# Moving two quarters of the position products, the last keys' projection and the axis exchange between two images of a hybrid attention kernel

## The chip, the cores and the metric

The kernel runs on one core of one Trainium2 chip. The metric is the device time of one execution in microseconds (us); the time given for a kernel is the median of its runs.

## The reference, cut to what matters

Eight images of 32 x 32 positions with 384 channels pass through two layers. Layer 0 is attention over all 1024 positions of an image with six heads of 64, with a position term for rows and one for columns added to the scores; layer 1 is causal attention and a feed-forward. The part that the change touches is layer 0's:

```
x = x + _L0_conv_ref(_gn(x), ...)
qkv = x.reshape(b, hw, c) @ qkv_w + qkv_b
attn = jnp.einsum('bqd,bkd->bqk', q * SCALE, k)
rel_h = jnp.einsum('bhwc,hkc->bhwk', r_q, Rh)
rel_w = jnp.einsum('bhwc,wkc->bhwk', r_q, Rw)
attn = attn + rel_h[:, :, :, :, None] + rel_w[:, :, :, None, :]
attn = jax.nn.softmax(attn, axis=-1)
```

and, at the end of an image, the feed-forward of layer 1:

```
h = x @ w_fc.T
h = jax.nn.gelu(h, approximate=False)
out = h @ w_proj.T
```

## The kernel before, in words

The order of the work is written out by hand, one instruction list for each engine, with semaphores between them. The eight images go one after the other. Matrices are kept as a float16 high part and a float16 low part, so most products are three matmuls.

One image is: position and value products of layer 0, its attention, its output projection, the normalisation and projections of layer 1, its attention, its output projection, and the feed-forward. The next image's layer 0 projections of queries and keys are laid into the feed-forward of this one, because there the tensor engine would wait for the gelus. This stretch between two attentions, called the seam here, occurs seven times.

In the seam the work before the change is this.

- `pair_products` (L555) makes two heads' queries or keys: 18 matmuls of 512 columns into two banks of PSUM. There are six pairs, 0 to 2 queries and 3 to 5 keys. Pairs 0 to 2 come before the feed-forward's twelve steps, pairs 3 to 5 are cut in pieces of five matmuls (`FILL`) and put one piece behind each `up` (L1303). ScalarE takes a pair out as its high part (`pair_high`, L574, two instructions), VectorE as its low part (`pair_low`, L591, two instructions).
- `turn_all` (L617) on GpSimd makes copies of the queries with the image's two axes exchanged: 12 instructions, which start when both parts of a pair are there.
- The feed-forward: `up`, `gelu` (L1315) on ScalarE, `down` (L1323), then for either half `o2_out` (L1329, VectorE), `spread` (L1337, PE), two `widen` (L1352, VectorE) and two `add` (L1358, GpSimd).
- `rel_products` (L653) are the position products, in four quarters of 96 small matmuls. Each quarter is taken out by four `rel_high` (L670) on ScalarE and four `rel_low` (L676) on VectorE. The first quarter waits for the low parts of all six pairs, and one quarter is put behind each of the value products 0 to 3.
- `v_products` (L688, L693) are the values, eight tiles of nine matmuls and a bias; `v_high` (L700, L701) on ScalarE and `v_low` (L705) on GpSimd take them out.
- The largest scores of head 0: 16 products `use("max", 0, n)` (L825), each followed by a reduction on VectorE (`release`, L971). They wait for 14 of the 16 `rel_low`, and use four banks in turn. Then `combine` (L1006, VectorE) puts the two halves together, a small matmul (L830) and a copy (L979) turn the result to a row, and a DMA (L1063) puts it beside the queries.
- Behind the row's matmul stand the last value product, the last two `rel_low`, and then the scores (`score_tiles`, L861, L863, L872) and the exponentials (L947), which begin the attention proper.

The exponential needs another table in ScalarE than the gelu. It is loaded where the first exponential stands.

Of the kernel before, what the change touches and what calls it, by code (L numbers as in the profile page):

```python
# [514 lines left out]
class Projections:  # L515

    COUNTS = (dict(mm=6, hi=12, lo=12, turned_hi=6, turned_lo=6, rel_mm=4, rel_hi=16, rel_lo=16, v_mm=8, v32=8, v_lo=8), dict(mm=6, hi=12, lo=12, v_mm=8, v32=8, v_lo=8))
# [60 lines left out]
    def pair_low(self, dve, i, heads=(0, 1)):  # L578
        nc, m, s, layer = self.nc, self.m, self.s, self.layer
        f = self.order[i]  # L580
        for e in heads:
# [17 lines left out]
            last.then_inc(s["lo"], 1)  # L599

    def copy_queries(self, sp, p):
# [28 lines left out]

    def rel_out(self, n):

        return self.m.ps[:, 2 * (1 - n % 2):2 * (1 - n % 2) + 2, :].rearrange("p k (i c) -> p (k i) c", c=P)[:, :, 0:NPAIR * IMG]

    def rel_products(self, pe, n):

        nc, m, s = self.nc, self.m, self.s
        if n >= 2:
            pe.wait_ge(s["rel_lo"], s.at("rel_lo", 4 * (n - 1)))
# [72 lines left out]
class Attention:  # L712
# [6 lines left out]
    def __init__(self, nc, m, layer, s, proj, norm=None, next_in=None):  # L719
# [47 lines left out]
        self.beside_v = (0, 0, 0, 2, 8, 14, 20, 25, len(self.prologue)) if self.causal else (0, 0, 0, 0, 0, 0, 6, len(self.prologue))  # L767
# [7 lines left out]
        ahead = (4, 5, 0, 1, 2, 3) if self.causal else (4, 5, 2, 3)  # L775
        self.banks = [ahead[r % len(ahead)] if r < len(self.prologue) else 4 + r % 2 for r in range(len(self.index))]
# [69 lines left out]
    def score_tiles(self, pe, i):  # L846
# [5 lines left out]
        sl = slot(h)  # L852
        if i >= 2:
# [15 lines left out]
        if g == 0:  # L869
            pe.wait_ge(s["row"], s.at("row", 16 * (h + 1)))  # L870
        for j in range(2):
# [67 lines left out]

    def scalar(self, act):  # L940
        nc, m, s = self.nc, self.m, self.s
        for i in range(self.N):
            w = self.cols(i)
            act.wait_ge(s["scores"], s.at("scores", i + 1))
            if i >= RING:
# [427 lines left out]
def build(nc, x, qkv_w, qkv_b, proj_w, proj_b, rel_h, rel_w, wq, wk, wv, wo, bo, c_fc_1, c_fc_2, c_proj_1, c_proj_2, out):  # L1373
# [7 lines left out]
    with ExitStack() as ctx:  # L1381
# [11 lines left out]
        ff_s = Counters(nc, ctx, "ff", **FeedForward.COUNTS)  # L1393
        copies_s = Counters(nc, ctx, "copies", queries=16 * NH)
        work = []
        for b in range(images):
# [3 lines left out]
            if b:  # L1400
                w.qkv0.copied = copies_s.of(b - 1)
            if b == 0:
                w.qkv0.bank, w.qkv0.before = (6, 4, 2, 0, 4, 2), (0, 0, 0, 0, 4, 6)
            w.with_v = ((0,), (1,), (2,), (3,), (), (), (), ()) if b else ((), (), (0,), (1,), (2,), (3,), (), ())
# [12 lines left out]
        REL_ORDER = list(range(16))  # L1417
# [4 lines left out]
        FILL = (0, 5, 5, 5, 5, 5, 5, 5, 5, 5, 5, 4)  # L1422
        HIGHS = (1, 2, 4, 5, 8, 9, 11, 11)
# [3 lines left out]
        def tensor(pe, w, before):  # L1427
            qkv0, attn0, proj0, ln, qkv1, attn1, proj1, ff = w.qkv0, w.attn0, w.proj0, w.ln, w.qkv1, w.attn1, w.proj1, w.ff
            for t in range(NT - 1):
                if not before or t > 0:  # L1430
                    qkv0.v_products(pe, t)
                for n in w.with_v[t]:
                    if n == 0:
                        pe.wait_ge(qkv0.s["lo"], qkv0.s.at("lo", 2 * PAIRS))
                    if before and n == 1:
                        pe.wait_ge(before.ff.s["widened"], before.ff.s.at("widened", 4))
                    qkv0.rel_products(pe, n)
                if t == 5 and not before:
                    prologue.ready(pe)
                if t == 5:  # L1440
                    pe.wait_ge(qkv0.s["rel_lo"], qkv0.s.at("rel_lo", RELS - 2))
                for u in attn0.prologue_part(t):
                    attn0.use(pe, u)
# [211 lines left out]
```

## Time and profile before

| | |
|---|---|
| median of three runs | 2883.28 us (2877.95 to 2890.47) |
| the profiled execution | 2876.72 us |
| its span | 2874.7 us |
| TensorE busy | 2648.2 us (92%) |
| VectorE busy | 1987.1 us (69%) |
| ScalarE busy | 2047.1 us (71%) |
| GpSimd busy | 1734.9 us (60%) |

Busy times are from the profile's page. Matmuls overlap in it, so 92% doesn't mean that TensorE works at its peak. The profile is of one execution, which was the shortest of those shown here, 6.6 us under the median. L with a number is a line of the kernel before; PE, DVE, ACT, POOL and SP are TensorE, VectorE, ScalarE, GpSimd and the queue that issues the DMAs.

### The profile page before, as it was taken

What the parts mean: (1) busy time and instruction counts of PE and PEld (TensorE: products, weight loads), DVE (VectorE), ACT (ScalarE), POOL (GpSimd) and SP (SyncE); (2) the same over time, 40 slices, a digit from 0 to 9 for tenths busy, and PEclk for the clock granted to TensorE, in tenths of its full rate; (3) what the DMA queues carried; (4) which work ended last, traced back from release to release, by engine and by line L of the source; (5) the groups of instructions that cost most, each with busy time, mean ns of one, the idle gap of its engine ahead of it and who ended that gap; (6) DMA issues with size and microseconds to landing.
All of it is one profiled execution on the core that took longest, in us unless ns stands there. A gap on an engine that the chain in (4) does not pass through costs nothing.

```text
span 2874.7 us, 69176 instructions
## 1 busy us (share of the span) xinstructions
PE 2648.2 (92%) x29116; PEld 1548.0 (54%) x29116; DVE 1987.1 (69%) x3631; ACT 2047.1 (71%) x2435; POOL 1734.9 (60%) x1181
## 2 busy tenths in 40 slices
PE   7899998999989998999989999899998999989995
PEld 4465644656446563565635656366553655546562
DVE  7776767666775767757677576775777758677574
ACT  6686866858668586785767867678766777668683
POOL 5474764737657376573756746566565665657473
PEclk8999999999999999999999999999999999999998
DMA  3100011000100001000010000200002000010000
GB/s 113 36 2 1 2 34 45 2 1 2 56 23 2 1 2 56 23 2 1 2 57 23 2 1 6 74 2 2 1 9 71 2 2 1 12 45 2 1 2 22
DMA packets 36115, 53.65 MB, mean 19 GB/s; under 512 B 5824, under 2 KB 32704, under 8 KB 35808
## 3 DMA queue, kind: packets, MB, share of 16 engines
q1 hardware_dynamic: 34304, 48.64, 5.5%
q8 instruction: 231, 3.78, 0.5%
q10 hardware_dynamic: 1504, 0.61, 0.1%
q14 instruction: 76, 0.62, 0.1%
HBM read 30.95 MB, written 12.58 MB: 15 GB/s over the span
## 4 chain that ended last, share of the span: by engine, by line
PE 49%; POOL 16%; ACT 13%; issue 11%; DVE 9%; DMA 1%; POOLq 0%; ACTq 0%; DVEq 0%; SPq 0%
POOL pl L1013 15%; PE ps L555 12%; PE ps L902 7%; PE ps L688 4%; PE ps L861 4%; PE ps L872 4%; ACT p L947 4%; PE ps L825 4%; PE ps L1104 4%; DVE mxp L971 3%; PE ps L863 3%; ACT ph L933 3%; ACT qa L670 2%; PE ps L1303 2%; PE ps L1323 2%
## 5 line engine op out<-in xcount | busy, mean ns | idle before, releaser
L1013 POOL TENSOR_TENSOR pl<-p,ph 128x1024 f16<-128x1024 f32 (+2 forms) x672 | 1095.9, 1644 | 384.2 <-ACT ph L933 378.3
L971 DVE TENSOR_REDUCE mxp<-ps 128x1 f32<-128x512 f32 (+2 forms) x1344 | 779.4, 627 | 267.9 <-PE ps L825 263.3
L947 ACT ACTIVATE p<-ps 128x1024 f32<-128x1024 f32 (+1 forms) x672 | 640.3, 953 | 165.8 <-PE ps L872 165.0
L933 ACT ACTIVATE ph<-p 128x1024 f16<-128x1024 f32 (+1 forms) x672 | 669.3, 996 | 21.4
L902 PEld LDWEIGHTS ps<-v,ph 128*128 128x128 f16 x9600 | 506.2, 97 | 128.2 <-issue 27.6
L902 PE MATMUL ps<-v,ph 128*128 128x65 f16 (+1 forms) x9600 | 531.0, 194 | 17.0 <-POOL pl L1013 16.0
L902 PE MATMUL ps<-v,pl 128*128 128x65 f16 x4800 | 509.1, 192 | 0.0
L902 PEld LDWEIGHTS ps<-v,pl 128*128 128x128 f16 x4800 | 446.8, 99 | 0.0
L872 PE MATMUL ps<-qc,kc 65*128 65x512 f16 (+3 forms) x1344 | 380.0, 364 | 0.1
L1013 DVE TENSOR_TENSOR pl<-p,ph 128x512 f16<-128x512 f32 (+1 forms) x336 | 244.2, 727 | 184.3 <-ACT ph L933 183.0
L705 POOL TENSOR_TENSOR v<-o,v 128x384 f16<-128x384 f32 x128 | 116.7, 918 | 411.0 <-ACT o L701 411.0
L861 PE MATMUL ps<-qa,ka 128*128 128x512 f16 x768 | 292.5, 381 | 0.0
L863 PE MATMUL ps<-qb,ka 128*128 128x512 f16 x768 | 291.7, 380 | 0.0
L825 PE MATMUL ps<-ka,qa 128*128 128x512 f16 x768 | 247.1, 383 | 43.9 <-DVE mxp L971 25.1
L700 ACT ACTIVATE v<-ps 128x384 f16<-128x384 f32 x128 | 63.6, 497 | 180.8 <-PE ps L693 107.3
L872 PEld LDWEIGHTS ps<-qc,kc 65*128 65x128 f16 (+1 forms) x1344 | 123.8, 98 | 126.4 <-issue 0.5
L825 PEld LDWEIGHTS ps<-ka,qa 128*128 128x128 f16 x768 | 73.2, 97 | 182.7 <-DVE mxp L971 70.8
L861 PE MATMUL ps<-qa,qb 128*128 128x512 f16 (+1 forms) x576 | 162.0, 344 | 2.1 <-ACT p L947 2.1
L555 PE MATMUL ps<-xin,wqkv_hi 128*128 128x512 f16 x576 | 155.9, 384 | 4.0 <-DVE xin L508 2.2
L825 PE MATMUL ps<-qb,qa 128*128 128x512 f16 (+2 forms) x576 | 154.9, 325 | 0.0
L1000 DVE TENSOR_TENSOR lT<-ps,hT 128x512 f16<-128x512 f32 x96 | 66.4, 692 | 127.5 <-ACT hT L938 127.5
L1315 ACT ACTIVATE p<-ps 128x1024 f32<-128x1024 f32 x96 | 98.0, 1021 | 60.6 <-PE ps L1303 59.5
(187 smaller groups left out, 5075.2 us busy)
## 6 DMA issues: line engine op xcount, KB each, us to landing
xin<-in_x SPq DMA_DIRECT2D x8, 1536.0 KB, 6.9
x<-in_x SPq DMA_DIRECT2D x8, 1536.0 KB, 8.1
out<-x SPq DMA_DIRECT2D x16, 768.0 KB, 4.1
qc<-qa SPq DMA_DIRECT2D x42, 128.0 KB, 2.3
p<-in_L_conv_qkv_w SPq DMA_DIRECT2D x3, 576.0 KB, 10.6
qc<-rowt SPq DMA_DIRECT2D x96, 2.0 KB
x<-in_L_attn_Wq SPq DMA_DIRECT2D x1, 576.0 KB, 7.9
x<-in_L_attn_Wk SPq DMA_DIRECT2D x1, 576.0 KB, 9.0
```

The lines of the kernel that those rows point to most:

```text
L555: mm = nc.tensor.matmul(m.ps[:, self.bank[i] + j, :], w[:, k, self.order[i] * P:(self.order[i] + 1) * P], x(k, 4 * j, 4 * j + 4), start=(n ...
L688: mm = nc.tensor.matmul(m.ps[:, 6 + t % 2, 0:C], flat_tile(x(k, t, t + 1)), w[:, k, 2 * C:3 * C], start=(n == 0), stop=(self.layer == 1 an ...
L705: self.nc.gpsimd.tensor_tensor(self.m.v[:, t, :, HD + 1:VW], self.m.o[:, t, :].rearrange("p (h d) -> p h d", d=HD), self.m.v[:, t, :, 0:HD ...
L825: mm = nc.tensor.matmul(m.ps[:, bank, 0:w], m.qa[:, sl, qt * P:(qt + 1) * P], self.ka[:, sl, kh * BANK:kh * BANK + w], start=not diag, sto ...
L861: nc.tensor.matmul(outs[j], self.ka[:, sl, keys[j]], m.qa[:, sl, q], start=True, stop=False)
L863: nc.tensor.matmul(outs[j], self.ka[:, sl, keys[j]], m.qb[:, sl, q], start=False, stop=False)
L872: mm = nc.tensor.matmul(outs[j], m.kc[crows(h), sl, keys[j]], m.qc[crows(h), sl, q], start=False, stop=True)
L902: mm = nc.tensor.matmul(m.ps[:, 6 + half % 2, c0:c0 + w], e, v, start=(first and n == 0), stop=(g in self.last_of_half and n == len(work) ...
L933: self.nc.scalar.activation(m.ph[:, i % RING, :, 0:w], m.p32[:, i % RING, :, 0:w], ACT.Copy).then_inc(self.s["hi"], 1)
L947: nc.scalar.activation(m.p32[:, i % RING, :, 0:w], m.ps[:, 2 * (i % 2):2 * (i % 2) + 2, 0:w], ACT.Exp, scale=SCALE).then_inc(s["exp"], 1)
L971: nc.vector.reduce_max(m.mxp[:, h % 2, kh, qt:qt + 1], m.ps[:, bank, 0:w], AX.X).then_inc(s["free"], 1)
L1013: engine.tensor_tensor(m.pl[:, i % RING, part, 0:w], m.p32[:, i % RING, part, 0:w], m.ph[:, i % RING, part, 0:w], ALU.subtract).then_inc(s ...
```

## The change

1. Pair 5 (the keys of heads 4 and 5) leaves the feed-forward. Its 18 matmuls are put, two at a time, behind the first nine of head 0's products for the largest scores, and value product 5 behind the next three. `FILL` has four matmuls a step in place of five, nine times.
2. ScalarE takes pair 5 out twice: as high part, and whole in float32 into a piece of `p32` that the exponentials don't use yet. GpSimd subtracts the two (two instructions) for the low part, behind `v_low` 5. The second scores wait until the bank is read, the fourth exponential and heads 4 and 5 until the low part is there.
3. Quarters 0 and 1 of the position products go into the feed-forward's end, with banks of their own. The first value product's pieces move ahead too. Quarters 2 and 3 follow value products 1 and 2. ScalarE's `rel_high` 0 to 3 and VectorE's `rel_low` 0 to 3 move with them.
4. The largest scores of head 0 use two banks in place of four, begin after 12 `rel_low`, and stand together. Value product 6 comes behind them, in the first image too.
5. `turn_all` starts when the layer's last small normalisation is done, and goes by the high parts first.
6. The first `spread` stands a step earlier; the exponential's table is asked for behind `v_high` 4.

```
-        self.bank = (4, 6, 2, 4, 2, 4) if layer == 0 else (0, 2, 4, 6, 0, 2)
-        self.before = (0, 0, 0, 2, 6, 8) if layer == 0 else (0, 0, 0, 0, 2, 4)
+        self.bank = (4, 6, 2, 4, 2, 2) if layer == 0 else (0, 2, 4, 6, 0, 2)
+        self.before = (0, 0, 0, 2, 6, 0) if layer == 0 else (0, 0, 0, 0, 2, 4)
+        self.late = None
...
+    def last_keys_out(self, act):
+
+        i = 2 * NPAIR - 1
+        f = self.order[i]
+        self.pair_high(act, i)
+        self.nc.scalar.activation(self.held_keys(), self.out2(i), ACT.Identity, bias=self.m.bqk[:, f:f + 1]).then_inc(self.late["whole"], 1)
+
+    def held_keys(self):
+        return self.m.p32[:, RING - 1, :, :].rearrange("p a b -> p (a b)")
+
+    def last_keys_low(self, pool, done):
+        m = self.m
+        pool.wait_ge(self.late["whole"], self.late.at("whole", 1))
+        pool.wait_ge(self.s["v_lo"], self.s.at("v_lo", done))
+        for h in (NH - 2, NH - 1):
+            self.nc.gpsimd.tensor_tensor(m.kc[own(h), slot(h), :], self.held_keys()[own(h), :], self.ka[own(h), slot(h), :],
+                                         ALU.subtract).then_inc(self.s["late_lo"], 1)
+        pool.wait_ge(self.s["late_lo"], self.s.at("late_lo", 2))
...
-        for p in range(NPAIR):
-            pool.wait_ge(s["lo"], s.at("lo", 2 * p + 2))
-            for part in range(2):
-                for parity in range(2):
-                    self.turn(pool, part, p, parity)
+        for part, p in ((0, 0), (0, 1), (1, 0), (1, 1), (0, 2), (1, 2)):
+            ready = ("hi", "lo")[part]
+            pool.wait_ge(s[ready], s.at(ready, 2 * p + 2))
+            for parity in range(2):
+                self.turn(pool, part, p, parity)
...
-        ahead = (4, 5, 0, 1, 2, 3) if self.causal else (4, 5, 2, 3)
-        self.banks = [ahead[r % len(ahead)] if r < len(self.prologue) else 4 + r % 2 for r in range(len(self.index))]
+        ahead = (4, 5, 0, 1, 2, 3) if self.causal else (0, 1)
+        first = len(self.prologue) + (not self.causal)
+        self.banks = [ahead[r % len(ahead)] if r < first else 4 + r % 2 for r in range(len(self.index))]
...
-            w.with_v = ((0,), (1,), (2,), (3,), (), (), (), ()) if b else ((), (), (0,), (1,), (2,), (3,), (), ())
+            w.with_v = ((1,), (2,), (3,), (), (), (), (), ()) if b else ((), (), (0,), (1,), (2,), (3,), (), ())
...
-        FILL = (0, 5, 5, 5, 5, 5, 5, 5, 5, 5, 5, 4)
-        HIGHS = (1, 2, 4, 5, 8, 9, 11, 11)
+        FILL = (0, 4, 4, 4, 4, 4, 4, 4, 4, 4, 0, 0)
+        HIGHS = (1, 2, 5, 6, 9, 10)
+        BESIDE_MAX = 9
...
+            pe.wait_ge(qkv0.s["rel_hi"], qkv0.s.at("rel_hi", RELS))
+            pe.wait_ge(qkv0.s["rel_lo"], qkv0.s.at("rel_lo", RELS - 4))
+            for u in attn0.prologue:
+                attn0.use(pe, u)
+                n = u[2]
+                if before and n < BESIDE_MAX:
+                    qkv0.pair_products(pe, PAIRS - 1, part=(EACH * n // BESIDE_MAX, EACH * (n + 1) // BESIDE_MAX))
+                elif before and n < BESIDE_MAX + NC_:
+                    qkv0.v_products(pe, NT - 3, [n - BESIDE_MAX])
+            qkv0.v_products(pe, NT - 2)
...
+                if i == 10 and w.next:
+                    pe.wait_ge(ff.s["widened"], ff.s.at("widened", 2))
+                    after.v_products(pe, 0, range(NC_ - 1))
+                if i == 11 and w.next:
+                    pe.wait_ge(after.s["lo"], after.s.at("lo", 2 * PAIRS - 4))
+                    after.rel_products(pe, 0)
...
-                if i == 9:
+                if i == 8:
                     ff.spread(pe, 0)
             if w.next:
-                pe.wait_ge(ff.s["widened"], ff.s.at("widened", 2))
-                after.v_products(pe, 0, range(NC_ - 1))
+                after.v_products(pe, 0, range(NC_ - 1, NC_))
             ff.down(pe, ff.PAIRS - 1)
             if w.next:
-                after.v_products(pe, 0, range(NC_ - 1, NC_))
+                pe.wait_ge(after.s["lo"], after.s.at("lo", 2 * PAIRS - 2))
+                after.rel_products(pe, 1)
             ff.spread(pe, 1)
...
+                if t == 4:
+                    attn0.table(act)
+                    if before:
+                        qkv0.last_keys_out(act)
...
-            low(4, (0,))
             ff.widen(dve, 0)
             ff.widen(dve, 1)
-            low(4, (1,))
-            low(5, (0,))
+            low(4)
             ff.o2_out(dve, 1)
-            low(5, (1,))
+            if w.next:
+                w.next.qkv0.rel_low(dve, 0)
             ff.widen(dve, 2)
             ff.widen(dve, 3)
+            if w.next:
+                for r in range(1, 4):
+                    w.next.qkv0.rel_low(dve, r)
```

## Rows read from the trace of the kernel before

**Rows 1.** The chain that ended last, first seam: start us, length us, what.

```profile
418.91 0.69 issue
...
420.94 1.23 PE ps L653 x96
...
439.79 1.46 PE ps L688 x9
441.25 0.27 PE ps L693
...
448.88 2.99 PE ps L688 x9
451.88 0.43 PE ps L693
```

**Rows 2.** The timeline of ACT, first seam: start us, length us, engine, line, operation.

```profile
422.20 3.28 ACT L670 ACTIVATE qa<-ps 32x768 f16<-32x768 f32 x4 [1.62 <-PE ps L653]
...
453.23 1.28 ACT L947 ACT_TABLE_LOAD   x1
454.53 1.02 ACT L947 ACTIVATE p<-ps 128x1024 f32<-128x1024 f32 x1
```

**Rows 3.** The timeline of DVE, same stretch.

```profile
421.79 0.95 DVE L1352 TENSOR_TENSOR pl<-ps,cp 128x768 f32<-128x768 f32 x1
423.03 3.91 DVE L676 TENSOR_TENSOR qb<-ps,qa 32x768 f16<-32x768 f32 x4 [0.29 <-ACT qa L670]
...
438.05 9.90 DVE L971 TENSOR_REDUCE mxp<-ps 128x1 f32<-128x512 f32 x16 [0.49 <-PE ps L825]
447.99 0.17 DVE L1006 TENSOR_TENSOR mxp<-mxp 128x8 f32<-128x8 f32 x1
448.92 0.28 DVE L979 CAST rowt<-ps 8x128 f16<-8x128 f32 x1 [0.77 <-PE ps L830]
```

**Rows 4.** The timeline of PE, same stretch, from a feed-forward step to the scores.

```profile
412.55 0.60 PE L1303 MATMUL ps<-ph,c 96*128 96x512 f16 x2
...
419.62 1.08 PE L1337 MATMUL ps<-spread,pl 128*128 128x32 f32 x8
...
439.40 0.39 PE L825 MATMUL ps<-ka,qa 128*128 128x512 f16 x1 [0.21 <-DVE mxp L971]
...
452.24 0.58 PE L861 MATMUL ps<-qa,ka 128*128 128x512 f16 x1
```

**Rows 5.** The chain again, one feed-forward step: `down`, `up`, five matmuls of a pair.

```profile
406.37 1.00 PE ps L1323 x8
...
407.90 1.08 PE ps L555 x5
```

**Rows 6.** The timeline of POOL, first and last of six pairs of `turn`.

```profile
391.88 3.93 POOL L617 TENSOR_SCALAR hT<-qa 64x1024 f16<-64x1024 f16 x2 [7.36 <-DVE qb L591]
...
411.84 3.92 POOL L617 TENSOR_SCALAR lT<-qb 64x1024 f16<-64x1024 f16 x2
```

**Rows 7.** Windows, PE alone: stretch, length, busy, granted clock (1.00 is full), DMA, GB/s.

```profile
428.00:430.00 2.00, 1.42 (x98) 1.00 0.39 136
444.00:446.00 2.00, 1.37 (x4) 0.96 0.00 0
...
446.00:453.00 7.00, 4.75 (x16) 0.52 0.00 0
...
2555.40:2562.40 7.00, 4.75 (x17) 0.76 0.01 3
```

**Rows 8.** The timelines of POOL and DVE inside the attention, 467 to 471 us.

```profile
467.68 2.13 POOL L1013 TENSOR_TENSOR pl<-p,ph 128x1024 f16<-128x1024 f32 x1 [1.37 <-ACT ph L933]
468.23 1.60 DVE L1006 TENSOR_TENSOR mxp<-mxp 128x8 f32<-128x8 f32 x1
```

**Rows 9.** The timeline of PE in the third seam, a stop inside a quarter.

```profile
1129.46 0.21 PE L653 MATMUL ps<-qa,rel_lo 64*32 64x96 f16 x1 [1.53 <-issue]
```

More of the change, by code:

```diff
@@ L598, in pair_low @@
                 last = nc.vector.tensor_copy(self.ka[other(h), slot(h), :], src[own(h), slot(h), :])
-            last.then_inc(s["lo"], 1)
+            if layer == 0 and i == 2 * NPAIR - 1:
+                last.then_inc(s["late_lo"], 1)
+            else:
+                last.then_inc(s["lo"], 1)
     def copy_queries(self, sp, p):
@@ L852, in score_tiles @@
         sl = slot(h)
+        if i == 1 and self.layer == 0 and self.proj.late:
+            pe.wait_ge(self.proj.late["whole"], self.proj.late.at("whole", 1))
         if i >= 2:
@@ L870, in score_tiles @@
             pe.wait_ge(s["row"], s.at("row", 16 * (h + 1)))
+        if g == 0 and self.layer == 0 and h == NH - 2:
+            pe.wait_ge(self.proj.s["late_lo"], self.proj.s.at("late_lo", 2))
         for j in range(2):
@@ L938, in ot_high, with table @@
         self.nc.scalar.activation(self.m.hT[:, c, hf * BANK:(hf + 1) * BANK], self.m.ps[:, self.bank(u), :], ACT.Copy).then_inc(self.s["ot_hi"], 1)
+    def table(self, act):
+        self.nc.scalar.activation(self.m.idle[:, :], self.m.bqk[:, 0:1], ACT.Exp, scale=0.0)
     def scalar(self, act):
@@ L944, in scalar @@
             act.wait_ge(s["scores"], s.at("scores", i + 1))
+            if i == RING - 1 and self.layer == 0 and self.proj.late:
+                act.wait_ge(self.proj.s["late_lo"], self.proj.s.at("late_lo", 2))
             if i >= RING:
@@ L1428, in tensor @@
             qkv0, attn0, proj0, ln, qkv1, attn1, proj1, ff = w.qkv0, w.attn0, w.proj0, w.ln, w.qkv1, w.attn1, w.proj1, w.ff
-            for t in range(NT - 1):
+            for t in range(NT - 3):
                 if not before or t > 0:
@@ L1433, in tensor @@
                     if n == 0:
-                        pe.wait_ge(qkv0.s["lo"], qkv0.s.at("lo", 2 * PAIRS))
+                        pe.wait_ge(qkv0.s["lo"], qkv0.s.at("lo", 2 * PAIRS - 2))
+                        pe.wait_ge(qkv0.s["late_lo"], qkv0.s.at("late_lo", 2))
                     if before and n == 1:
+                        continue
+                    if before and n == 2:
                         pe.wait_ge(before.ff.s["widened"], before.ff.s.at("widened", 4))
                     qkv0.rel_products(pe, n)
[L1438 to L1443, printed above, removed]
+            if not before:
+                prologue.ready(pe)
+                qkv0.v_products(pe, NT - 3)
+                qkv0.rel_products(pe, 3)
+            pe.wait_ge(qkv0.s["rel_hi"], qkv0.s.at("rel_hi", RELS))
[8 more added lines that the diff above has]
+            qkv0.v_products(pe, NT - 2)
             def beside_row():
@@ L1525, in scalar, with vector @@
                         w.next.qkv0.pair_high(act, 2 + n // 2, (n % 2,))
-        def vector(dve, w):
+            if w.next:
+                for r in range(4):
+                    w.next.qkv0.rel_high(act, r)
+        def vector(dve, w, before):
             qkv0, attn0, proj0, ln, qkv1, attn1, ff = w.qkv0, w.attn0, w.proj0, w.ln, w.qkv1, w.attn1, w.ff
-            for r in REL_ORDER[:-2]:
+            for r in range(4 if before else 0, RELS - 2):
                 qkv0.rel_low(dve, r)
@@ L1534, in after_row @@
             def after_row():
-                for r in REL_ORDER[-2:]:
+                for r in range(RELS - 2, RELS):
                     qkv0.rel_low(dve, r)
@@ L1569, in gpsimd @@
                 qkv0.v_low(pool, t)
+                if t == 5 and before:
+                    qkv0.last_keys_low(pool, t + 1)
             attn0.gpsimd(pool, proj0.bias_tiles)
@@ L1612, in _ @@
                 prologue.scalar(act)
-                for w in work:
-                    scalar(act, w)
+                for b, w in enumerate(work):
+                    scalar(act, w, work[b - 1] if b else None)
             @block.vector
@@ L1618, in _ @@
                 prologue.vector(dve)
-                for w in work:
-                    vector(dve, w)
+                for b, w in enumerate(work):
+                    vector(dve, w, work[b - 1] if b else None)
             @block.gpsimd
@@ L1624, in _ @@
                 prologue.gpsimd(pool)
-                for w in work:
-                    gpsimd(pool, w)
+                for b, w in enumerate(work):
+                    gpsimd(pool, w, work[b - 1] if b else None)
             @block.sync
```

21 lines of the change are left out of this document (13 added, 8 removed).

## The prediction

> **What bounds the kernel now.** I read the profile's page first: PE is busy 92% of the span, so a saving has to come from stretches in which PE waits. The change touches the seam between two images, so I followed the chain of waits through the first seam, 390 to 460 us, and then laid the engines' timelines beside each other. The other six seams look alike; three of them lose another 0.4 to 1 us in the position products.
>
> The chain leaves PE at 420.9. Quarter 0 of the position products takes 1.23 us to its first reader [rows 1], and from then on ScalarE goes without a gap until 438.07: four `rel_high` of 0.82 us and a value tile of 0.9 us make 4.2 us a quarter, four times [rows 2]. VectorE follows 0.3 us behind, does its 14th `rel_low` at 437.57, and starts the 16 reductions at 438.05 [rows 3]. They take 9.90 us, one every 0.61 us. In them PE does one matmul for each and waits for VectorE [rows 4], and its granted clock falls from 1.00 to 0.50 (2.4 to 1.2 GHz) at 446 us: a mean of 0.52 over the next 7 us [rows 7]. So value product 7 takes 2.99 + 0.43 us, where value product 5 needs 1.46 + 0.27 us at the full clock [rows 1]. The scores begin at 452.24 [rows 4], the first exponential at 454.53, held by the table load that ends there [rows 2]. The reader should see three things in turn: ScalarE's 16.8 us, VectorE's 9.9 us, and PE at half speed.
>
> **The feed-forward's end.** Nine steps lose a matmul: five take 1.08 us [rows 5], so nine are 1.94 us. Steps with a `down` are bound by PE and keep that gain; steps without are bound by the round `up`, gelu, `up` of 1.71 us (412.55 to 414.26) and PE now waits 0.2 us in them. `up` 10, at 412.55 before [rows 4], comes at 410.6 to 410.8. `up` 11 follows 1.71 us later, at 412.4. Then PE has 0.43 (`up`), 1.1 (quarter 0), 1.0 (`down` [rows 5]), 0.7 (the rest of value product 0), 1.0 (`down`), 1.1 (quarter 1), and comes to the second `spread` at 417.75, before at 419.62 [rows 4]: 1.9 us earlier, although two quarters now lie ahead of it. One reason is that the stop of 0.69 us for `o2_out` [rows 1] is filled by quarter 1. The earlier first `spread` costs nothing: its `o2_out` is done 0.5 us before.
>
> Are quarter 0's inputs there at 412.8? `turn_all` waited 7.36 us for `pair_low` and ran from 391.88 to 415.76, 12 x 1.99 us [rows 6]. It now starts at 386.1, when the small normalisation is done, and ends at 410.0. That is 2.8 us before quarter 0, so the earlier start is needed and is just enough. It has no price on VectorE, whose instructions there read PSUM.
>
> **The position products.** ScalarE begins them at about 414.6 and has its 16 `rel_high` and three value tiles done at 430.7, no longer the bound. VectorE is: one `rel_low` lies before the last two `widen`, which end at 420.85 (before 422.74 [rows 3]); 13 more at 3.91 / 4 = 0.98 us [rows 3] end at 433.6. The reductions start at 433.65 in place of 438.05: **4.4 us**.
>
> **The largest scores.** With two banks product n waits for reduction n-2. From a reduction's end to PE's start are 0.13 us and the product takes 0.39 us [rows 4], together under the 0.61 us of a reduction, so two banks alone cost nothing. But PE now has three matmuls of 0.216 us a step, 0.65 us, seven times; then three steps with a third of value product 5, 2.4 us; then four at 0.61 us. Set out from the first reduction, the last ends at 10.55 us, not 9.90. Value product 6 runs from 9.7 to 11.4, so the row's matmul waits for it until 11.4 (in place of 10.3). Copy until 12.1, two `rel_low` of 0.98 us until 14.05, and the scores start at **14.05**; value product 7, at the full clock, is done at 13.4 under them. Before it was 452.24 - 438.05 = 14.19 us. The scores' first half also ran at the slow clock, 0.3 us. The table load is under cover; since the scores' later steps follow PE and not the first exponential, its 0.6 us count for nothing. Sum with nothing in the way: 4.4 + 0.1 + 0.3 = **4.8 us a seam**.
>
> **What is in the way.** *The clock.* PE is idle from 429.0 to 431.8 and from 433.1 to 434.4, waiting for `rel_low`. Before, PE was busy 1.42 of 2 us there [rows 7] and kept the full clock; the clock fell behind the reductions, with PE busy 1.37 of 2 us and then waiting for `combine` [rows 7]. I expect it to fall as the reductions start. At half clock a step is 1.30 us, not 0.65, so each slow microsecond costs half of one. Means of 0.52 and 0.76 over 7 us [rows 7] are 6.8 and 3.4 us at half clock in the first and the last seam, and part of the new one lies in PE's idle time. Bounds 0 and 3.4 us; I take **0.85 us** for 1.7 us of exposure.
>
> *The port.* Pair 5 is out of PE 5.3 us behind the first reduction. ScalarE then has 1.11 + 1.13 + 1.1 us and the value tile 0.97, until 9.8; GpSimd `v_low` 5 until 10.7, and then the two new subtractions of some 2.1 us each (2.13 us for 128 x 1024 [rows 8]). `combine` is due at 10.6. Inside the attention `combine`, 0.17 us alone [rows 3], began at 468.23 while GpSimd subtracted two SBUF operands, and ended with it: 1.60 us [rows 8]. So `combine` waits for `v_low` 5 or, if it comes a few tenths late, for the first new subtraction, until 12.9: 1.8 us on the path. My walk isn't good to 0.2 us; I take half, **0.9 us**, with bounds 0 and 1.8.
>
> The Trainium skill, "SBUF — State Buffer", section "Who interferes with whom", gives a rule for this: a VectorE instruction with two SBUF inputs and a GpSimd one that reads SBUF shut each other out for a whole instruction, and the first to start wins. By that rule a seam gains either 3.95 or 2.15 us and nothing between, as one engine or the other comes first. The trace agrees: `combine` ended when GpSimd did [rows 8].
>
> Late keys elsewhere: GpSimd ends them at 15.0 and its last `v_low` at 16.8, before the first exponentials' low part is due (about 17.7); the fourth exponential is due later still. The second scores wait for ScalarE's third reading at 8.8, done. On SP nothing changes its order: the query copies still follow `pair_high`, and the stores and the load of x come 2 us earlier. The last image has no next one to fill its feed-forward; there only the first `spread` moves, ahead of work that waits for gelus, so its end stays.
>
> *The first image* has no products beside its reductions: it starts them when it did, but value product 6 now stands between them and the row instead of among them. At the clock that fell there it takes 3.4 us, partly beside the last reduction; on the other side a gap of 0.6 us among the reductions goes. I take 0.7 us lost, bounds -1 and 1.5.
>
> **Sum.** 4.8 - 0.85 - 0.9 = 3.05 us a seam, 21.4 us in seven, less 0.7: 20.7 us. From the profiled 2876.7 us that is 2856; the median stands 6.6 us above that execution, so 2862.6 for a median like it. I give 2861. What a measurement of this kernel can tell from no change is about 0.5%, 14.4 us.
>
> **Rivals.**
> - *Clean*: PE keeps its clock and `combine` comes first. 7 x 4.8 - 0.7 = 33 us, 2850 us (2844 beside the profiled execution). For it: PE is full once the reductions run. Against: 4 us of idle time just before. Chance 0.2.
> - *Port every time*: `combine` always meets the new subtraction: 7 x 2.15 - 0.7 = 14.4 us, 2869 us. For it: the schedule repeats, so it may well be all seven or none. Chance 0.2.
> - *Quarters that stop*: PE stood 1.53 us inside a quarter in the third seam, waiting for nothing the profile shows [rows 9]. Two quarters now lie on PE's way to the last `spread`, and through `widen` on VectorE's. Two such stops a seam take 3 us, which with the clock leaves less than 1 us a seam: 2878 us, no change. Against: only three seams showed stops, all late in the stretch. Chance 0.12, with whatever else hides the gain.
> - *Slower*: the clock stays low from the first reduction to the scores. Ten steps then take 13.8 us, not 6.9, value products 6 and 7 3.4 us each, and the scores start 24 us behind the first reduction: 10 us lost against 4.8 won, 7 x 5.2 = 37 us, 2920 us. It decides from 9.6 us of slow clock on. Against it: the longest such stretch is 6.8 us, and PE is busy throughout. Chance 0.05.
>
> The forecast itself has 0.43. Faster by over 0.5% are it, clean, and two thirds of the port case: 0.76; within 0.5% 0.19; slower 0.05. The range takes in clean, from 2845, and reaches to the port case with a slow clock of full length, 2875.
>
> **What would show it.** Right: first reduction about 15 us behind the second `spread`, not 18; 16 reductions in 10.5 to 12 us; a `combine` of 0.2 to 2.1 us; value product 7 in 1.7 us; no table load before the first exponential. Wrong: gaps on VectorE between `rel_low`s (then ScalarE or PE bounds), PE waiting for `turn` at quarter 0, a granted clock of 0.50 beyond 5 us in the reductions, or `combine` late for value product 5.

## The result, and the profile after

The changed kernel takes 2852.81 us (median of four runs, 2849.44 to 2853.7), the kernel before beside it on the same chip 2880.61 (2876.35 to 2890.47): a ratio of 0.9899 with a 95% interval of 0.9881 to 0.9917. The forecast was 2861 us in a range of 2845 to 2875, faster with a chance of 0.76. It came out faster by 1.0%, inside the range and 8 us below the forecast. The two profiled executions have spans of 2874.7 and 2849.7 us: 25.0 us less, where the steps of the forecast summed to 20.7.

The page's first part, of the kernel after:

```profile
span 2849.7 us, 69244 instructions
...
PE 2638.5 (93%) x29116; PEld 1547.0 (54%) x29116; DVE 1973.6 (69%) x3617; ACT 2058.2 (72%) x2450; POOL 1763.1 (62%) x1195
```

Busy times have hardly moved: PE has 10 us less, GpSimd 28 us more (the late keys' subtractions). What went is waiting. The timeline of ACT in the first seam (start us, length us, engine, line; L695 is `rel_high`, L617 the late keys' second reading, L983 the exponential):

```profile
414.73 3.28 ACT L695 ACTIVATE qa<-ps 32x768 f16<-32x768 f32 x4
...
427.34 3.28 ACT L695 ACTIVATE qa<-ps 32x768 f16<-32x768 f32 x4
...
432.31 1.28 ACT L972 ACT_TABLE_LOAD   x1
...
439.74 2.24 ACT L575 ACTIVATE ka<-ps,bqk 64x1024 f16<-64x1024 f32 x2 [5.94 <-PE ps L556]
442.01 1.11 ACT L617 ACTIVATE p<-ps,bqk 128x1024 f32<-128x1024 f32 x1
...
449.94 1.02 ACT L983 ACTIVATE p<-ps 128x1024 f32<-128x1024 f32 x1 [0.98 <-PE ps L902]
...
453.23 1.02 ACT L983 ACTIVATE p<-ps 128x1024 f32<-128x1024 f32 x1 [1.17 <-PE ps L902]
```

ScalarE starts its 16 readings 7.5 us earlier than in [rows 2] and is done at 430.62, 3.4 us ahead of the reductions. The table load stands before the late keys' reading, and the first exponential now waits for PE, not for it. The timeline of DVE, same stretch (L701 is `rel_low`, L1007 the reductions, L1042 `combine`, L1015 the row's copy):

```profile
417.95 0.95 DVE L701 TENSOR_TENSOR qb<-ps,qa 32x768 f16<-32x768 f32 x1
...
420.21 0.95 DVE L1388 TENSOR_TENSOR pl<-ps,cp 128x768 f32<-128x768 f32 x1
421.19 12.79 DVE L701 TENSOR_TENSOR qb<-ps,qa 32x768 f16<-32x768 f32 x13
434.01 8.04 DVE L1007 TENSOR_REDUCE mxp<-ps 128x1 f32<-128x512 f32 x12
442.44 2.48 DVE L1007 TENSOR_REDUCE mxp<-ps 128x1 f32<-128x512 f32 x4 [0.38 <-PE ps L851]
444.95 0.17 DVE L1042 TENSOR_TENSOR mxp<-mxp 128x8 f32<-128x8 f32 x1
446.25 0.28 DVE L1015 CAST rowt<-ps 8x128 f16<-8x128 f32 x1 [1.13 <-PE ps L856]
```

The 13 `rel_low` run back to back: VectorE is the bound, as the working said. The first reduction starts at 434.01, before at 438.05 [rows 3]; the 16 take 10.91 us, before 9.90. GpSimd's timeline (L640 the turn, L730 `v_low`, L627 the late keys' subtractions) shows how close the port came:

```profile
387.25 7.87 POOL L640 TENSOR_SCALAR hT<-qa 64x1024 f16<-64x1024 f16 x4 [1.64 <-issue]
...
407.22 3.92 POOL L640 TENSOR_SCALAR lT<-qb 64x1024 f16<-64x1024 f16 x2
...
443.96 0.88 POOL L730 TENSOR_TENSOR v<-o,v 128x384 f16<-128x384 f32 x1 [10.63 <-ACT o L726]
444.99 4.32 POOL L627 TENSOR_TENSOR kc<-p,ka 64x1024 f16<-64x1024 f32 x2
```

`combine` began at 444.95, the subtraction at 444.99. It came 0.04 us ahead and took 0.17 us, in this seam and in the other six. That is a fixed distance, not the same near miss seven times: in six traces whose order of work is the same here (the changed kernel twice, and the runs below with the quarters back, the old turn, the late table load and the filler) it is 0.03 or 0.04 us in all 42 seams, while `combine` itself comes anywhere from 10.71 to 13.39 us behind the first reduction. In these traces both sides follow PE: ScalarE starts its readings when the late keys' last matmul is done and GpSimd follows ScalarE, and the 13th reduction waits 0.38 us for a product that stands behind value product 5. No run moved the one without the other to test this, except the delayed `combine` below. PE, the quarter's first matmul, the row's and the scores' first:

```profile
413.11 0.22 PE L678 MATMUL ps<-qa,rel_hi 64*32 64x96 f16 x2
...
445.83 0.39 PE L856 MATMUL ps<-minus,mxp 128*8 128x128 f32 x2
...
448.43 0.39 PE L889 MATMUL ps<-qa,ka 128*128 128x512 f16 x1 [0.39 <-DVE qb L701]
```

**Where the 25 us are.** I cut each seam at three marks that both traces have: the narrow input of the next image's projections (`x2_high`), the first reduction, and the second exponential of the first head. Means over the seven seams, in us, from the timelines:

| | before | after | gained, all seams |
|---|---|---|---|
| narrow input to first reduction | 52.89 | 49.53 | 23.5 |
| first reduction to second exponential | 18.87 | 19.31 | -3.0 |
| the rest of the image | six 279.9, last 268.2 | six 279.1, last 267.9 | 5.0 |
| first image, to its narrow input | 384.33 | 385.43 | -1.1 |
| behind the last narrow input | 40.3 | 39.7 | 0.6 |

That sums to 25.0. The third line was in no step of the forecast. It is the clock. The table is of one execution of each kernel, and the first image alone is not sure to 2 us: in a second trace of the changed kernel it takes 387.72 us. Other executions of the kernel before lose more clock: on one chip they go from 2874.17 us at a granted clock of 0.982 to 2888.29 at 0.973, the changed kernel's beside them only from 2848.87 to 2854.46 at 0.982 to 0.980. So in the difference of the medians, 27.8 us, the clock has probably a larger part than here; no run separates it. Windows of PE alone, after (stretch, length, busy, granted clock, DMA, GB/s):

```profile
432.00:436.00 4.00, 3.86 (x11) 0.59 0.46 163
436.00:443.00 7.00, 6.61 (x33) 1.00 0.00 0
443.00:450.00 7.00, 6.22 (x32) 1.00 0.11 15
739.60:743.00 3.40, 3.40 (x10) 0.58 0.00 0
780.60:784.00 3.40, 3.40 (x11) 0.58 0.32 112
```

and before:

```profile
798.00:805.00 7.00, 5.17 (x17) 0.55 0.01 2
955.00:959.00 4.00, 3.66 (x14) 0.65 0.02 4
```

Before, the clock fell to 1.2 GHz behind the reductions (3.4 us in five seams, 6.8 in two, as 798 to 805) and again some 218 us behind the narrow input, in the second layer (955), in all images but the last. After, both are gone. In their place it falls as the reductions start (432, 780), and in six of seven seams also some 7 us behind the narrow input (739.6), where before it did so in the first seam only. The second trace of the changed kernel has the same two low stretches in the same seams, and none at 218 us.

### The profile page after: what moved, and what is told of

It reads as the page before. It is cut to its first block, busy times and chain, and to the rows that moved or that the text cites. A ratio compares the mean times of both kernels' runs of the same rounds, so it can differ in the third digit from the quotient of the medians.

```text
span 2849.7 us, 69244 instructions
## 1 busy us (share of the span) xinstructions
PE 2638.5 (93%) x29116; PEld 1547.0 (54%) x29116; DVE 1973.6 (69%) x3617; ACT 2058.2 (72%) x2450; POOL 1763.1 (62%) x1195
## 4 chain that ended last, share of the span: by engine, by line
PE 51%; POOL 16%; ACT 12%; issue 11%; DVE 10%; DMA 0%; POOLq 0%; ACTq 0%; DVEq 0%; SPq 0%
POOL pl L1049 15%; PE ps L556 12%; PE ps L932 7%; PE ps L851 5%; PE ps L889 4%; PE ps L902 4%; PE ps L713 4%; ACT p L983 4%; PE ps L1140 4%; DVE qb L701 3%; PE ps L891 3%; ACT ph L963 3%; PE ps L1339 2%; ACT p L1351 2%; PE ps L1359 2%
## 5 line engine op out<-in xcount | busy, mean ns | idle before, releaser
L1007 DVE TENSOR_REDUCE mxp<-ps 128x1 f32<-128x512 f32 (+2 forms) x1344 | 784.0, 626 | 258.8 <-PE ps L851 253.0
L983 ACT ACTIVATE p<-ps 128x1024 f32<-128x1024 f32 (+1 forms) x672 | 641.0, 954 | 175.8 <-PE ps L902 175.0
L730 POOL TENSOR_TENSOR v<-o,v 128x384 f16<-128x384 f32 x128 | 116.1, 918 | 369.3 <-ACT o L726 368.7
L851 PE MATMUL ps<-ka,qa 128*128 128x512 f16 x768 | 260.5, 392 | 54.9 <-DVE mxp L1007 22.3
L556 PE MATMUL ps<-xin,wqkv_hi 128*128 128x512 f16 x576 | 167.5, 404 | 2.5 <-DVE xin L508 2.2
```

Source lines behind the costliest of these rows:

```text
L556: mm = nc.tensor.matmul(m.ps[:, self.bank[i] + j, :], w[:, k, self.order[i] * P:(self.order[i] + 1) * P], x(k, 4 * j, 4 * j + 4), start=(n ...
L730: self.nc.gpsimd.tensor_tensor(self.m.v[:, t, :, HD + 1:VW], self.m.o[:, t, :].rearrange("p (h d) -> p h d", d=HD), self.m.v[:, t, :, 0:HD ...
L851: mm = nc.tensor.matmul(m.ps[:, bank, 0:w], m.qa[:, sl, qt * P:(qt + 1) * P], self.ka[:, sl, kh * BANK:kh * BANK + w], start=not diag, sto ...
L983: nc.scalar.activation(m.p32[:, i % RING, :, 0:w], m.ps[:, 2 * (i % 2):2 * (i % 2) + 2, 0:w], ACT.Exp, scale=SCALE).then_inc(s["exp"], 1)
L1007: nc.vector.reduce_max(m.mxp[:, h % 2, kh, qt:qt + 1], m.ps[:, bank, 0:w], AX.X).then_inc(s["free"], 1)
```

## The experiments

Each is the changed kernel with one edit, unless it says otherwise. "R0" is the first reduction.

**Quarters 0 and 1 back behind the last `spread`**, with everything else of the change kept.

```diff
-            w.with_v = ((1,), (2,), (3,), (), (), (), (), ()) if b else ((), (), (0,), (1,), (2,), (3,), (), ())
+            w.with_v = ((0,), (1,), (2,), (3,), (), (), (), ()) if b else ((), (), (0,), (1,), (2,), (3,), (), ())
...
-                    after.rel_products(pe, 0)
...
-                after.rel_products(pe, 1)
...
-                for r in range(4):
-                    w.next.qkv0.rel_high(act, r)
...
-            for r in range(4 if before else 0, RELS - 2):
+            for r in range(RELS - 2):
...
-                w.next.qkv0.rel_low(dve, 0)
...
-                for r in range(1, 4):
-                    w.next.qkv0.rel_low(dve, r)
```

> The changed kernel with the two quarters of the position products put back behind value products 0 and 1; the late keys and the rest stay. My theory (the start of the reductions sets the gain, and ScalarE's 16 rel_high of 0.82 us in a row bound it as before): ScalarE begins its first rel_high behind the second spread, at about 420 us of the first seam and not at 414.7, the reductions start 3.1 us later than in the changed kernel, 7 x 3.1 = 22 us more, span about 2871 us. Rival (the gain is from pair 5 being out of the feed-forward, the quarters only follow it): under 1 us a seam, span 2850 to 2856 us.

Median 2875.1 us, ratio to before 0.9984 (0.9974 to 0.9994), span 2870.7: 21.0 us above the changed kernel. The total is as forecast, its make-up is not: the start of the reductions was to come 3.1 us later a seam and came 1.2 later, which is 8.3 us of the 21.0. Timeline of DVE, first seam:

```profile
430.16 1.95 DVE L701 TENSOR_TENSOR qb<-ps,qa 32x768 f16<-32x768 f32 x2 [0.29 <-ACT qa L695]
...
433.26 0.69 DVE L1007 TENSOR_REDUCE mxp<-ps 128x1 f32<-128x512 f32 x1 [1.15 <-PE ps L851]
434.54 0.69 DVE L1007 TENSOR_REDUCE mxp<-ps 128x1 f32<-128x512 f32 x1 [0.59 <-PE ps L851]
```

`rel_low` follows `rel_high` again (0.29 us), and the first reductions wait 1.15 and 0.59 us for PE, which was idle for 4.69 us ahead of them (2.87 in the changed kernel): in six seams its clock is then low for 6.8 us, not 3.4. R0 is at 50.71 against 49.53, and the second exponential comes another 1.6 us later behind it (20.90 against 19.31): 11.1 us in seven seams. What is left against before is 4 us in all. R0 itself is still 2.2 us a seam ahead of the kernel before; the wait for PE and the longer low stretch behind it give nearly all of that back. So without the two quarters, the rest of the change is worth next to nothing in time.

**The last keys' projection back at the feed-forward's end**, quarters kept, their banks changed over and the waits to match.

```diff
-        self.bank = (4, 6, 2, 4, 2, 2) if layer == 0 else (0, 2, 4, 6, 0, 2)
+        self.bank = (4, 6, 2, 4, 2, 4) if layer == 0 else (0, 2, 4, 6, 0, 2)
...
-        FILL = (0, 4, 4, 4, 4, 4, 4, 4, 4, 4, 0, 0)
-        HIGHS = (1, 2, 5, 6, 9, 10)
-        BESIDE_MAX = 9
+        FILL = (0, 5, 5, 5, 5, 5, 5, 5, 5, 5, 5, 4)
+        HIGHS = (1, 2, 4, 5, 8, 9, 11, 11)
+        BESIDE_MAX = 0
...
-                    if before:
-                        qkv0.last_keys_out(act)
...
-                    qkv0.last_keys_low(pool, t + 1)
...
+            low(5)
```

> The changed kernel with pair 5 back in the feed-forward (five matmuls a step again, its low part on VectorE), and the two quarters still at the feed-forward's end, their banks changed over so that quarter 0 needs pairs 0 to 4 only and quarter 1 all six. My theory: PE has 18 x 0.216 = 3.9 us more before the second spread, less the 0.2 us stops in four steps, and VectorE two pair_low of 1.29 us; the 16 reductions take 10.3 us and not 10.9. Sum 2.5 to 3.5 us a seam, 18 to 25 us more, span 2868 to 2874 us. Rival (the matmuls of pair 5 cost as much beside the reductions as in the feed-forward, so its place is worth nothing): 0 to 0.5 us a seam.

Median 2878.24 us, ratio 0.9999 (0.9986 to 1.0012), span 2879.1: 29.4 us above the changed kernel, more than forecast. R0 is 2.0 us later a seam, 14.1 us in all, as the filled steps say. Another 4.7 us come between R0 and the second exponential, 7.0 in the rest of the images and 3.6 in the first image and at the end; for the most part that is the clock. Without the late keys' matmuls between the largest scores PE waits 0.21 us or more ahead of each of the last ten products. Timeline of DVE, first seam:

```profile
441.93 8.06 DVE L1007 TENSOR_REDUCE mxp<-ps 128x1 f32<-128x512 f32 x13 [0.90 <-PE ps L851]
...
452.54 0.28 DVE L1015 CAST rowt<-ps 8x128 f16<-8x128 f32 x1 [2.34 <-PE ps L856]
```

The clock is low at the reductions' start in all seams and again behind them in five, and at 218 us (207 in the last image) in the second layer in all. With the clock low behind the reductions the row's copy waits 2.34 us, in this seam, and the rest of the image is 1.0 us longer in the mean. So both parts are needed: the quarters alone, like the keys alone, leave the kernel within 0.2% of before.

**The turn in its old order**, `pair_low` waited for pair by pair.

```diff
-        for part, p in ((0, 0), (0, 1), (1, 0), (1, 1), (0, 2), (1, 2)):
-            ready = ("hi", "lo")[part]
-            pool.wait_ge(s[ready], s.at(ready, 2 * p + 2))
-            for parity in range(2):
-                self.turn(pool, part, p, parity)
+        for p in range(NPAIR):
+            pool.wait_ge(s["lo"], s.at("lo", 2 * p + 2))
+            for part in range(2):
+                for parity in range(2):
+                    self.turn(pool, part, p, parity)
```

> The changed kernel with the exchange of axes in its old order, each pair waiting for its low part. My theory: the 12 turns run from 392.9 (the first pair's low part) for 12 x 1.99 us until 416.8, not until 411.1, quarter 0 waits for them from 413.1 to 416.9, and all behind it on PE is 3.8 us later: 7 x 3.8 = 27 us more, span about 2876 us, no better than the kernel before. Rival (quarter 0 has slack, because ScalarE or VectorE bound what follows): under 1.5 us a seam.

One execution: 2898.43 us, span 2896.7, 47 us above the changed kernel, where 27 were forecast. The turn begins 5.6 us later (392.90) and quarter 0 waits for it. Timeline of PE:

```profile
416.99 0.22 PE L678 MATMUL ps<-qa,rel_hi 64*32 64x96 f16 x2 [4.01 <-POOL lT L640]
```

R0 is 4.9 us later a seam (54.44), 1.5 later than in the kernel before, for 3.8 forecast. I had not counted that PE, idle for four microseconds, loses its clock: a further low stretch lies some 32 us behind the narrow input in every seam, of 3.4 us in five and of 6.8 in two. The early turn is what makes the early quarters possible.

**Combine a little later**: two small reductions ahead of it, with no use but time.

```diff
+        if h == 0 and self.layer == 0:
+            for j in range(2):
+                nc.vector.reduce_max(m.rs[:, 1, j:j + 1], m.mxp[:, 0, 1, 0:4], AX.X)
         nc.vector.tensor_tensor(m.mxp[:, h % 2, 0, both], m.mxp[:, h % 2, 0, both], m.mxp[:, h % 2, 1, both], ALU.max).then_inc(s["combined"], 1)
```

> The changed kernel with two small reductions (0.17 us each) ahead of head 0's combine on VectorE, so that GpSimd's first subtraction of the late keys, which started 0.04 us behind combine, starts before it. My theory (the two lock each other out for a whole instruction): combine takes about 2 us, the row's matmul comes 1.3 to 1.5 us later, 9 to 12 us more in all, span 2859 to 2862 us. Rival (no lock; only the added 0.34 us, which value product 6 on PE covers): combine stays at 0.17 us and the span within 1.5 us of 2849.7.

One execution: 2886.86 us, span 2885.1: 35 us lost, not 9 to 12. The lock itself is as forecast. Timeline of DVE, and behind it of POOL:

```profile
448.05 0.22 DVE L1044 TENSOR_REDUCE rs<-mxp 128x1 f32<-128x4 f32 x2
448.19 2.04 DVE L1045 TENSOR_TENSOR mxp<-mxp 128x8 f32<-128x8 f32 x1
450.79 0.28 DVE L1015 CAST rowt<-ps 8x128 f16<-8x128 f32 x1 [0.56 <-PE ps L856]
```

```profile
448.08 4.31 POOL L627 TENSOR_TENSOR kc<-p,ka 64x1024 f16<-64x1024 f32 x2
```

`combine` is now 0.11 us behind the subtraction and takes 2.04 us in all seven seams, not 0.17. The rule quoted ahead from the Trainium skill, "SBUF — State Buffer", section "Who interferes with whom", agrees with this: the first to start keeps the other out for its whole instruction, and `combine` ends when the subtraction does. Beside `combine`, part of value product 6 was waited for anyway (1.13 us ahead of the copy in the changed kernel, 0.56 here), so the copy comes 1.5 to 1.6 us later in the three seams where the low stretch lies about as it did: 10 to 11 us in seven. The other 24 are the clock, as far as they can be placed. In three seams the low stretch at the reductions grows to 6.8 us and the copy comes at 16.0 instead of 13.9; the rest of the image is 8.2 us longer in all; and the last image's feed-forward runs at 1.2 GHz to the end, 7.8 us more. The first image is 3.1 us longer, but of that 2.3 us lie between two traces of the changed kernel too. With a single execution, how much of the 24 the delay brought on is not shown. Windows of PE:

```profile
2834.80:2884.00 49.20, 28.71 (x96) 0.50 0.08 30
```

**Value products 5 and 6 spread out among the reductions**, 16 of the late keys' matmuls put into PE's wait for the last `rel_low`, and GpSimd held after the subtractions until `combine` is done.

```diff
-        BESIDE_MAX = 9
+        AHEAD = 16
+        V5, V6 = (2, 4, 7), (9, 11, 13)
...
+            if before:
+                pe.wait_ge(qkv0.s["rel_lo"], qkv0.s.at("rel_lo", 8))
+                qkv0.pair_products(pe, PAIRS - 1, part=(0, AHEAD))
...
-                if t == 5 and before:
+                if t == 4 and before:
                     qkv0.last_keys_low(pool, t + 1)
+                    pool.wait_ge(attn0.s["combined"], attn0.s.at("combined", 1))
```

> The changed kernel with its second stretch laid out by what the traces showed: 16 of pair 5's 18 matmuls go into the 2.9 us in which PE waits for rel_low ahead of the reductions, the last two behind product 0, a third of value product 5 behind products 2, 4 and 7, a third of value product 6 behind 9, 11 and 13; GpSimd makes the late keys' low part ahead of v_low 5, and v_low 5 to 7 wait for combine. My theory: PE has no idle stretch ahead of the reductions, so the clock stays at 1.00 there; they take 10.0 us, not 11.0, combine meets no subtraction, the row's matmul waits for nothing, and the row's copy comes at 10.8 us behind the first reduction, not at 12.35. 1.5 us a seam and as much in the first image: span about 2838 us. Rival (the clock's low stretches move with any change of the period, as in the kernel with the later combine, and cost elsewhere what they leave here): the span within 5 us of 2849.7 or above, with low stretches at other places of each image.

Median 2846.93 us (2842.22 to 2853.26), ratio 0.9871 (0.9853 to 0.9889), span 2843.8, 5.9 us below the changed kernel but not the 2838 expected. Timelines of DVE and of POOL in the second seam:

```profile
788.39 1.29 DVE L1007 TENSOR_REDUCE mxp<-ps 128x1 f32<-128x512 f32 x2 [0.28 <-PE ps L851]
789.72 0.17 DVE L1042 TENSOR_TENSOR mxp<-mxp 128x8 f32<-128x8 f32 x1
790.44 0.28 DVE L1015 CAST rowt<-ps 8x128 f16<-8x128 f32 x1 [0.56 <-PE ps L856]
```

```profile
782.18 4.31 POOL L627 TENSOR_TENSOR kc<-p,ka 64x1024 f16<-64x1024 f32 x2 [3.82 <-ACT p L617]
790.01 1.74 POOL L730 TENSOR_TENSOR v<-o,v 128x384 f16<-128x384 f32 x2 [3.52 <-DVE mxp L1042]
```

GpSimd's subtractions end 3.2 us before `combine`, and the row waits 0.56 us, not 1.13, since no value product stands whole ahead of it. The second exponential comes at 18.40 in six seams (19.55 in one), 0.7 us sooner in the mean than the changed kernel's 19.31. The low stretch at the reductions is gone, and that at 7 us is left in two seams; one at some 213 us (203 in the last image) is back in five of seven, and the rest of the images is 5.1 us longer for it. That is what the rival foretold in part. The edit has three parts, and this run does not tell them apart.

**Only the 12 matmuls in the gap**, three steps of two more, nothing else moved.

```diff
-        BESIDE_MAX = 9
+        AHEAD = 12
+        BESIDE_MAX = 3
...
+            if before:
+                pe.wait_ge(qkv0.s["rel_lo"], qkv0.s.at("rel_lo", 8))
+                qkv0.pair_products(pe, PAIRS - 1, part=(0, AHEAD))
...
-                    qkv0.pair_products(pe, PAIRS - 1, part=(EACH * n // BESIDE_MAX, EACH * (n + 1) // BESIDE_MAX))
+                    qkv0.pair_products(pe, PAIRS - 1, part=(AHEAD + 2 * n, AHEAD + 2 * n + 2))
```

> The changed kernel with 12 of pair 5's 18 matmuls in PE's wait ahead of the reductions, nothing else moved. My theory: the clock's low stretch at the start of the reductions goes, they take 10.2 us and not 11.0; but pair 5 is out 4 us earlier, so GpSimd's two subtractions run from about 7 to 11.2 us behind the first reduction and combine, due at 10.2, waits for the second of them: combine takes about 1 us, the row's copy stays at 11.8 to 12.3 us. Span 2845 to 2851 us. Rival (no lock): combine stays at 0.17 us and the copy comes at 11.6 us.

Median 2853.65 us, ratio 0.9892 (0.9875 to 0.9908), the changed kernel's. Now R0 is at 48.55 in all seven seams, with no low stretch at 7 or at 48 us. `combine` falls into the late keys' second subtraction and waits for its end, 0.38 to 0.55 us. Timeline of DVE, second seam:

```profile
793.45 0.40 DVE L1042 TENSOR_TENSOR mxp<-mxp 128x8 f32<-128x8 f32 x1
```

It is a miss all the same: the row's copy comes at 12.88, forecast at most 12.3, the second exponential is at 19.85, and the clock falls 57 and 214 us behind the narrow input instead. Two low stretches went and two others came.

**Without the early table load**, `attn0.table(act)` taken out.

```diff
-                if t == 4:
-                    attn0.table(act)
-                    if before:
-                        qkv0.last_keys_out(act)
+                if t == 4 and before:
+                    qkv0.last_keys_out(act)
```

> The changed kernel without the early request for the exponential's table, so that the load of 1.28 us stands ahead of the first exponential again. By my prediction it counts for nothing: ScalarE is free 1 us before the first exponential, which comes 0.3 us later, and the second exponential follows PE and stays at 19.3 us behind the first reduction. Span within 2 us of 2849.7, if the clock's low stretches stay where they are. Rival (the table is part of the gain): 1.28 us a seam, 9 us more.

One execution: 2853.16 us, span 2851.4, 1.7 above, which is less than two executions of the changed kernel differ by. The first exponential comes 0.4 us later (16.43), the second 0.1 (19.39): the early load counts for nearly nothing, as said.

**Filler matmuls in PE's wait**, with no use but to keep PE busy.

```diff
+            if before:
+                pe.wait_ge(qkv0.s["rel_lo"], qkv0.s.at("rel_lo", 8))
+                for n in range(12):
+                    nc.tensor.matmul(m.ps[:, 2 + n % 2, :], qkv0.wh[:, 0, 0:P], qkv0.high(0, 0, 4), start=True, stop=True)
```

> The changed kernel with 12 matmuls of 512 columns more in a seam, whose results nothing reads, in PE's wait ahead of the reductions; nothing is moved or removed. My theory: they cost nothing where they stand (2.6 us of a wait of 2.9), the clock does not fall at the reductions, and these take 10.6 us and not 11.0: 0.4 us a seam. What the kernel gains in all hangs on where else the clock now falls. Rival (the low stretch there costs 0.85 us a seam, as I forecast): reductions of 10.2 us.

One execution: 2851.25 us, span 2849.5, no change. It prices the low stretch at the reductions. Timeline of DVE, first seam:

```profile
436.75 7.81 DVE L1007 TENSOR_REDUCE mxp<-ps 128x1 f32<-128x512 f32 x12
...
447.46 0.17 DVE L1042 TENSOR_TENSOR mxp<-mxp 128x8 f32<-128x8 f32 x1
```

That stretch is gone in all seven seams; `combine` comes 10.71 us behind R0 in place of 11.03, and the second exponential 0.32 sooner (18.98). The low stretch there cost 0.3 us in the first trace of the changed kernel and 0.5 in the second (`combine` at 11.20), not the 0.85 that I took. The clock's records show on what the price depends: it is 0.23, 0.36, 0.45 and 0.60 us where 1.27, 1.51, 1.70 and 2.00 us of the low stretch lie behind R0. By my estimate from these four, the first 0.8 us behind R0 cost nothing, and from there on each slow microsecond costs half of one. What hides the total is elsewhere: the first image is 2.8 us longer than in the first trace, but the changed kernel timed again on this chip has 387.72 us there against 388.21, so that is no work of the filler. The rest of the images is 1.7 us longer.

**The changed and the spread-out kernel again**, on the same chip, with no edit.

> The changed kernel itself, timed beside the spread-out one on the same chip: 0.99 of the kernel before, as measured.

> The spread-out kernel once more: 0.987 of the kernel before, 4 to 6 us under the changed kernel timed beside it. If its gain were the luck of one chip, it would be within 2 us of the changed kernel here.

Changed: median 2851.92 us (2848.87 to 2854.46), ratio 0.9899 (0.9877 to 0.992). Spread out: 2847.64 (2843.39 to 2848.44), ratio 0.988 (0.9855 to 0.9904). The ranges of the two do not touch, though the intervals of their ratios do: about 4 us, 0.15%, in favour of the spread-out version, the fastest of those run.

## Why the prediction was right, and where not

- **Feed-forward's end and quarters: right.** The first seam starts 1.1 us later here, so the marks are read against the narrow input. Quarter 0 came 27.68 us behind it, forecast 28.5; the second `spread` and the first reduction followed as set out, 13 `rel_low` in 12.79 us, nothing late. The turn ended 2 us before quarter 0 needed it, and taking its early start away cost 4.01 us of waiting at once.
- **4.4 us to R0: too large.** The first seam gained 5.1 us (53.72 to 48.58), the seven in the mean 3.4. The term was worked from that seam alone, and there the kernel before had a low stretch at the start of the feed-forward that its other seams lack; after, it is the other six that have it. Between seams with a full clock and no stop in the position products the gain is 3.8 us (52.36 to 48.58). Three seams of the kernel before lost 0.4 to 1.2 us to such stops, which are gone. The step that failed is "The other six seams look alike". Such a stretch costs 1.1 us in the feed-forward (49.69 against 48.58 after), and it is named nowhere in the forecast.
- **Reductions in 10.55 us: right.** 10.67 with a full clock, 10.91 to 11.03 without. The scores began 14.42 us behind R0, forecast 14.05 with nothing in the way.
- **The clock, 0.85 us: right place, too large.** It fell as the reductions began, as said, for 3.4 us; but it cost 0.3 us (the filler's run), 0.5 in the second trace. The exposure of 1.7 us was a fair guess, 1.3 to 1.5 us lay behind R0; the price of half a microsecond for each was not, since the first 0.8 us cost nothing: seams with 1.70 us of exposure, in the second trace, lose 0.45. Its gain elsewhere was missed: 0.8 us in each of six images, from the low stretch in the second layer that no longer comes. That, 5.0 us with the last image's 0.3, is why the total was 25.0 and not 20.7.
- **The port, 0.9 us: wrong.** "I take half" stood between two outcomes that exclude one another, 0 and 1.8. The trace has 0 in all seven, by 0.04 us; the delayed `combine` has the other, 1.5 to 1.6 us on the path. That it came out as 0 and not 1.8 was luck: the walk wasn't good to 0.2 us. But the distance of the two is the same in every seam, so it is all or none, as the rival said. Nor is it "nothing between", as I put it: a `combine` that falls inside a subtraction waits for what is left of it, 0.4 us in the run with the gap filled.
- **First image, 0.7 us: 1.1, by another cause.** Value product 6 behind the reductions is visible (the copy waits 2.22 us in it), but its exponentials come 0.16 us later only. 0.94 us lies with a low stretch at 251 us which before doesn't have. I didn't test what brings it, and the first image's time differs by 2.3 us between two traces of the changed kernel, so this term is below what one trace can tell.
- **Rivals.** "Quarters that stop": in the seven seams PE stood inside a quarter once, for 0.25 us, in the sixth. "Slower": the clock is never low beyond 3.4 us in the reductions. "Clean": the port's half of it came true, the clock's didn't.
- **The sum** of the seam, 3.05 us forecast and 2.93 measured, agrees by offsets: 1.0 less to R0, 0.9 more behind it (-0.43 for -1.35). That agreement is luck.
- **The median.** I put it 6.6 us above the profiled execution, as for the kernel before. The changed kernel's is 0.8 above: its executions differ by 4.3 us, not by 14.1. These 5.8 us and the 4 us more that were gained, less the 1.6 us by which 2861 stands under the working's 2862.6, make the 8 us between forecast and result.

What stays open: why the clock falls where it does. The runs show that the low stretches move when the length of an image or its waits change (gap, filler, keys, quarters), not a rule by which their places could be foretold.

## What to carry to other kernels

Fill the engine that waits ahead of a bound stretch, and check with one run for each part whether the parts work alone: here neither the early quarters nor the moved projection is worth over 0.2% without the other. Filling PE's wait with other matmuls for the clock's sake gained nothing by itself (2851.25 and 2853.65 us). Where a tiny instruction on the path and a long one of GpSimd's meet within a few tenths of a microsecond, don't take the mean of both outcomes: order them by a semaphore, or expect the whole price or none, in every period alike. Read every seam of a periodic kernel before working from the first, and list its low-clock stretches with it, since a small delay can move them all.

## What was unexpected of the hardware

In the one execution of the kernel with a delay of 1.5 us in each of seven seams 35 us were lost, over three times the delay itself, while low-clock stretches grew and moved; in the last feed-forward 49 us ran at 0.50. A low stretch of 3.4 us cost 1.1 us at the feed-forward's start and 0.2 to 0.6 at the reductions', by how much of it lay behind their start. And two instructions 0.03 to 0.04 us apart kept that distance in all 42 seams of six traces, while both moved by up to 2.7 us against the first reduction.
